# The first expert stage of a two-layer transformer kernel: 32 pairs and 7 single tiles instead of 28 and 15, with a tile table of sixteen segments

## The reference

```
logits = einsum('btd,ed->bte', x, router_w)
top_vals, top_idx = top_k(logits, 2);  top_w = softmax(top_vals)
h = square(relu(einsum('nd,edh->enh', xf, w1)))
y = einsum('enh,ehd->end', h, w2)
out = sum over the two choices of top_w * y[choice, row]
x = x + attention0(layernorm(x)) + experts0(layernorm(x))
```

## Time and profile before

| | |
|---|---|
| median of 3 runs | 760.42 us (760.25, 760.42, 761.84) |
| span of the profiled execution | 761.9 us |
| TensorE busy | 716.6 us, 94% |
| VectorE busy | 564.2 us, 74% |
| ScalarE busy | 438.9 us, 58% |
| GpSimd busy | 456.4 us, 60% |
| share of TensorE in the chain that ended last | 84% |
| DMA | 113.96 MB, mean 150 GB/s |

### The profile page before, as it was taken

How to read it: one execution, slowest core, us unless ns; L and a number is a source line. 1 busy time by engine, 2 the same in 40 slices (tenths; PEclk the granted TensorE clock), 3 DMA queues, 4 the chain that set the end, 5 groups by cost and what they waited for, 6 DMA issues and landing times.

```text
span 761.9 us, 19272 instructions
## 1 busy us (share of the span) xinstructions
PE 716.6 (94%) x6112; PEld 631.8 (83%) x6112; DVE 564.2 (74%) x1280; ACT 438.9 (58%) x928; POOL 456.4 (60%) x577
## 2 busy tenths in 40 slices
PE   6999999799999999999998999899999899999994
PEld 4888864699999999999977999777778678888883
DVE  4888874788778887788758886589998766676632
ACT  5444525576776776755526888456677664544411
POOL 3676777889798696988422323024376645665363
PEclk9999999999999999999999999799999999999997
DMA  9799752343454344453168996145457755666342
GB/s 255 209 266 277 210 148 75 90 134 108 132 151 123 112 125 138 124 136 107 48 184 274 300 288 184 29 95 123 107 110 194 222 194 133 147 148 147 54 56 28
DMA packets 151103, 113.96 MB, mean 150 GB/s; under 512 B 59359, under 2 KB 141282, under 8 KB 151012
## 3 DMA queue, kind: packets, MB, share of 16 engines
q1 hardware_dynamic: 137812, 86.94, 41.0%
q0 software_dynamic: 12624, 25.35, 13.3%
q10 hardware_dynamic: 576, 0.53, 0.3%
HBM read 68.68 MB, written 40.80 MB: 144 GB/s over the span
## 4 chain that ended last, share of the span: by engine, by line
PE 84%; DVE 7%; issue 3%; ACT 2%; DMA 1%; POOL 1%; SPq 0%; POOLq 0%; DVEq 0%; ACTq 0%
PE banks L917 13%; PE bank L1173 11%; PE bank L882 11%; PE banks L1184 5%; PE bank L973 5%; PE banks L747 4%; PE banks L812 4%; PE bank L893 4%; PE bank L754 3%; PE bank L1080 3%; PE bank L1063 3%; PE banks L990 3%; PE bank L865 2%; PE bank L1052 2%; PE banks L801 2%
## 5 line engine op out<-in xcount | busy, mean ns | idle before, releaser
L917 PE MATMUL banks<-r_split,rt_split 128*128 x852 | 111.0, 285 | 1.1 <-issue 0.9
L917 PEld LDWEIGHTS banks<-r_split,rt_split 128*128 128x128 f32 x852 | 105.1, 191 | 1.9 <-issue 1.9
L2247 POOL DMA_INDIRECT ults_by_choice_and_token<-rw,y_id x71 | 79.1, 1114 | 45.1 <-ACT rw L1361 34.6
L1173 PE MATMUL bank<-r_split 128*128 128x512 f32 x384 | 89.6, 391 | 1.3 <-issue 1.1
L882 PE MATMUL bank<-wqkv_split,rt_split 128*128 128x256 f32 x560 | 86.9, 286 | 4.2 <-DVE rt_split L1767 4.1
L1173 PEld LDWEIGHTS bank<-r_split 128*128 128x128 f32 x384 | 71.4, 188 | 16.3 <-issue 1.9
L2346 POOL DMA_INDIRECT out_x<-r,idx x32 | 50.2, 1568 | 52.9 <-DVE r L2105 45.2
L882 PEld LDWEIGHTS bank<-wqkv_split,rt_split 128*128 128x128 f32 x560 | 76.0, 189 | 5.9 <-DVE rt_split L1767 5.4
L2216 POOL DMA_INDIRECT rows_by_expert<-rw,slots x64 | 68.0, 1062 | 18.6 <-issue 9.8
L1767 DVE TENSOR_TENSOR rt_split<-r,rt_split 128x512 fp32r<-128x512 f32 x56 | 62.1, 1149 | 18.7 <-ACT rt_split L1290 16.6
L1792 DVE TENSOR_TENSOR rt_split<-rw,rt_split 128x512 fp32r<-128x512 f32 x71 | 63.1, 919 | 6.3 <-ACT rt_split L1354 6.0
(11 more groups left out here) (275 smaller groups left out, 1759.3 us busy)
## 6 DMA issues: line engine op xcount, KB each, us to landing
rt<-in_w SPq DMA_DIRECT2D x24, 512.0 KB, 4.8
rw<-rows_by_expert SPq DMA_DIRECT2D x71, 128.0 KB
r<-in_w SPq DMA_DIRECT2D x16, 512.0 KB, 7.4
rt<-ults_by_choice_and_token SPq DMA_DIRECT2D x32, 256.0 KB, 4.1
rw<-in_x SPq DMA_DIRECT2D x16, 256.0 KB, 4.8
rw<-in_sin_q SPq DMA_DIRECT2D x32, 128.0 KB
rw<-x_layer SPq DMA_DIRECT2D x16, 256.0 KB
x_plus_bias<-rw SPq DMA_DIRECT2D x16, 256.0 KB, 3.5
```

The source lines that it names most:

```text
L917: last = pe.matmul(bank[6 + t % 2][:, 0:D], hidden_T(h, t, c), w[:, ds(e2, 1), o + c * D:o + (c + 1) * D], start=n == 0, stop=n == 3 * HC - 1)
L1173: last = pe.matmul(bank[2 * (hb % 2) + k][:, :], w[:, o:o + P], x[:, s.par, c, :], start=n == 0, stop=n == 3 * DC - 1)
L2247: pool.indirect_dma_start(y0_d[:, :], bass.IndirectOffsetOnAxis(y_id[:, t:t + 1].bitcast(I32), 0), c_y[:, t % XB, :], None, bounds_check=l ...
```

## The change

ND goes from 28 to 32: T1 is 64, there are 32 pairs and 7 singles. The table has sixteen segments: for each expert its full pairs, and then for each expert its odd tile counted as two places, the tile and an empty one behind it. The first 64 places are the pairs, what remains of the odd tiles is halved into singles. The chain on VectorE has 21 small operations where it had 15, its four comparisons and products work on 16 segments instead of 8, and so does the reduction. Each expert's end gets 256 rows of zeros instead of 128. Three memsets more run on GpSimd at the start. The split of the next layer's weights moves from T1 + 4 to T1 + 1 and from T1 + 6 to T1 + 3, that is from 60 to 65 and from 62 to 67.

```
--- before.py
+++ after.py
@@ -147,7 +147,6 @@
         xT_all = r3f[:, 0:DC * N].rearrange("p (c n) -> p c n", c=DC)
         v_all = r2[:, :].rearrange("p (h t n) -> p h t n", h=2, t=NT)
         pid0 = sb("pid0", [P, 1])
-        one8 = sb("one8", [P, E])
         m_all = sb("m_all", [P, NB, 2, D])
         hot1_hi = r3[:, 0:NT * E * 32].rearrange("p (c n) -> p c n", c=NT)
         hot1_lo = r3[:, NT * E * 32:NT * E * 64].rearrange("p (c j e m) -> p c j e m", c=NT, j=2, e=E)
@@ -184,15 +183,17 @@
         prod = scratch([TOPK * GT * E])
         upto, span_e = scratch([E]), scratch([GT * E], BF16)
         end_r = sb("end_r", [P, E], I32)
-        n_i, n_f, d_pair, d_one = scratch([3 * E], I32), scratch([E]), scratch([E]), scratch([E])
-        pair_n, pair_incl, u2, s_incl = scratch([E]), scratch([E]), scratch([E + 1]), scratch([E])
+        n_i, n_f = scratch([3 * E], I32), scratch([E])
+        seg, covered, one16 = scratch([2 * E]), scratch([2 * E]), scratch([2 * E])
+        seg_incl, start, apart = scratch([2 * E]), scratch([2 * E + 1]), scratch([2 * E])
+        step_to = scratch([2 * E])
         base_f, headmask = scratch([ST0]), scratch([2, P // 2])
         top_v, top_i = scratch([NT, E]), scratch([NT, E]).bitcast(U32)
         base_i = scratch([ST0], I32)
         assert taken[0] <= 2 * DC * H, taken[0]
         taken[0] = 2 * DC * H
         taken[0] += 8 * D
-        past, past_d = scratch([E, ST0]), scratch([E, ST0])
+        past = scratch([2 * E, ST0])
         taken[0] = 2 * DC * H
         a_kr, a_t, a_v = scratch([2, 2 * D]), scratch([2 * D]), scratch([3, 2 * D])
         o = taken[0]
@@ -302,7 +303,7 @@
         x1_out, x1_late = [sem(f"x1_stored_{i}") for i in range(4)], sem("last_x1_stored")
         xn1_out, xb1_out = sem2("xn1_stored"), sem2("xb1_stored")
 
-        XB, ND = 4, 28
+        XB, ND = 4, 32
         T1 = 2 * ND
         NTR = ST0 - ND
         c_xg = work([XB, D], reset=True)
@@ -563,8 +564,8 @@
                 load_xq(i)
             sp.wait_ge(table_r, 1)
             for e in range(0, E, 2):
-                r = sp.value_load(end_r[0:1, e:e + 1], min_val=0, max_val=(REG - 1) * P)
-                sp.dma_start(xs0_d[ds(r, P), :], zeros).then_inc(zero_out, 16)
+                r = sp.value_load(end_r[0:1, e:e + 1], min_val=0, max_val=(REG - 2) * P)
+                sp.dma_start(xs0_d[ds(r, 2 * P), :].rearrange("(j p) n -> p j n", p=P), over_mid(zeros, 2)).then_inc(zero_out, 16)
             for i in range(4):
                 sp.wait_ge(sc0_out[i], 16 * TOPK * GT * NG // 4)
             sp.wait_ge(table_r, 2)
@@ -1317,8 +1318,8 @@
             copy_q(0)
             act.wait_ge(table_r, 1)
             for e in range(1, E, 2):
-                r = act.value_load(end_r[0:1, e:e + 1], min_val=0, max_val=(REG - 1) * P)
-                act.dma_start(xs0_d[ds(r, P), :], zeros).then_inc(zero_out, 16)
+                r = act.value_load(end_r[0:1, e:e + 1], min_val=0, max_val=(REG - 2) * P)
+                act.dma_start(xs0_d[ds(r, 2 * P), :].rearrange("(j p) n -> p j n", p=P), over_mid(zeros, 2)).then_inc(zero_out, 16)
             for g in range(1, NQ):
                 if g == NQ - 1:
                     high_rows_T(0)
@@ -1385,7 +1386,7 @@
                 if t < ST0:
                     relu0(t)
                     high0(t)
-                if t == T1 + 4:
+                if t == T1 + 1:
                     act.wait_ge(consts_b, 16 * 9)
                     act.activation(wq1_hi[:, :, :], wqkv1_s[:, :, :], ACT.Copy).then_inc(wq1_r, 1)
 
@@ -1724,24 +1725,32 @@
             link(dve.tensor_scalar(n_i[:, E:2 * E], n_i[:, 0:E], 7, None, ALU.logical_shift_right))
             link(dve.tensor_scalar(n_i[:, 2 * E:3 * E], n_i[:, 0:E], 8, None, ALU.logical_shift_right))
             link(dve.tensor_copy(n_f, n_i[:, E:2 * E]))
-            link(dve.tensor_copy(pair_n, n_i[:, 2 * E:3 * E]))
-            link(dve.tensor_scalar(pair_n, pair_n, 2.0, None, ALU.mult))
-            link(dve.tensor_tensor_scan(pair_incl, one8[:, :], pair_n, 0.0, ALU.mult, ALU.add))
-            link(dve.tensor_tensor(u2[:, 0:E], pair_n, pair_incl, ALU.subtract))
-            link(dve.tensor_scalar(u2[:, 0:E], u2[:, 0:E], float(T1), 0.0, ALU.add, ALU.max))
-            link(dve.tensor_tensor(u2[:, 0:E], u2[:, 0:E], pair_n, ALU.min))
-            link(dve.memset(u2[:, E:E + 1], 0.0))
-            link(dve.tensor_tensor(d_one, n_f, u2[:, 0:E], ALU.subtract))
-            link(dve.tensor_tensor_scan(s_incl, one8[:, :], d_one, float(T1), ALU.mult, ALU.add))
-            link(dve.tensor_tensor(d_one, u2[:, 1:E + 1], n_f, ALU.subtract))
-            link(dve.tensor_scalar(d_one, d_one, float(SPAN), None, ALU.add))
-            link(dve.tensor_scalar(d_pair, pair_n, -1.0, float(SPAN), ALU.mult, ALU.add))
-            for lo, hi, incl, d in ((0, T1, pair_incl, d_pair), (T1, ST0, s_incl, d_one)):
-                link(dve.tensor_tensor(past[:, :, lo:hi], over_mid(iota_t[:, lo:hi], E), over_last(incl, hi - lo), ALU.is_ge))
-                link(dve.tensor_tensor(past_d[:, :, lo:hi], past[:, :, lo:hi], over_last(d, hi - lo), ALU.mult))
-            link(dve.tensor_reduce(base_f, past_d.rearrange("p e t -> p t e"), AX, ALU.add))
+
+
+
+            link(dve.tensor_scalar(seg[:, 0:E], n_i[:, 2 * E:3 * E], 2.0, None, ALU.mult))
+            link(dve.tensor_tensor(seg[:, E:2 * E], n_f, seg[:, 0:E], ALU.subtract))
+            link(dve.tensor_scalar(seg[:, E:2 * E], seg[:, E:2 * E], 2.0, None, ALU.mult))
+            link(dve.tensor_tensor_scan(seg_incl, one16, seg, 0.0, ALU.mult, ALU.add))
+            link(dve.tensor_tensor(covered, seg, seg_incl, ALU.subtract))
+            link(dve.tensor_scalar(covered, covered, float(T1), 0.0, ALU.add, ALU.max))
+            link(dve.tensor_tensor(covered, covered, seg, ALU.min))
+            link(dve.tensor_copy(start[:, E:2 * E], seg[:, 0:E]))
+            for part, lo, hi in (("pairs", 0, T1), ("singles", T1, ST0)):
+                if part == "singles":
+                    link(dve.tensor_copy(start[:, 0:E], covered[:, 0:E]))
+                    link(dve.tensor_tensor(seg, seg, covered, ALU.subtract))
+                    link(dve.tensor_scalar(seg[:, E:2 * E], seg[:, E:2 * E], 0.5, None, ALU.mult))
+                    link(dve.tensor_tensor_scan(seg_incl, one16, seg, float(T1), ALU.mult, ALU.add))
+                link(dve.tensor_tensor(step_to, start[:, 1:2 * E + 1], start[:, 0:2 * E], ALU.subtract))
+                link(dve.tensor_tensor(step_to, step_to, seg, ALU.subtract))
+                link(dve.tensor_tensor(step_to, step_to, apart, ALU.add))
+                link(dve.tensor_tensor(past[:, :, lo:hi], over_mid(iota_t[:, lo:hi], 2 * E), over_last(seg_incl, hi - lo),
+                                       ALU.is_ge))
+                link(dve.tensor_tensor(past[:, :, lo:hi], past[:, :, lo:hi], over_last(step_to, hi - lo), ALU.mult))
+            link(dve.tensor_reduce(base_f, past.rearrange("p e t -> p t e"), AX, ALU.add))
             link(dve.tensor_tensor(base_f, base_f, iota_t[:, :], ALU.add))
-            link(dve.tensor_scalar(base_f[:, T1:ST0], base_f[:, T1:ST0], u2[:, 0:1], -float(T1), ALU.add, ALU.add))
+            link(dve.tensor_scalar(base_f[:, T1:ST0], base_f[:, T1:ST0], start[:, 0:1], -float(T1), ALU.add, ALU.add))
             dve.tensor_scalar(tile_r[:, :], base_f, float(P), None, ALU.mult).then_inc(table_r, 1)
             link(dve.tensor_copy(base_i, base_f))
             link(dve.tensor_scalar(base_i, base_i, 6, None, ALU.logical_shift_right))
@@ -1825,7 +1834,7 @@
                     low0(t - 1)
                 if t < ST0:
                     square0(t)
-                if t == T1 + 6:
+                if t == T1 + 3:
                     dve.wait_ge(wq1_r, 1)
                     dve.tensor_tensor(wq1_lo[:, :, :], wqkv1_s[:, :, :], wq1_hi[:, :, :].bitcast(F32), ALU.subtract)\
                        .then_inc(wq1_r, 1)
@@ -2176,7 +2185,10 @@
             pool.iota(span_e, pattern=[[0, GT], [SPAN, E]], base=0, channel_multiplier=0, allow_small_or_imprecise_dtypes=True)
             pool.iota(upto, pattern=[[-SPAN * P, E]], base=P - 1, channel_multiplier=0, allow_small_or_imprecise_dtypes=True)
             pool.iota(iota_t[:, :], pattern=[[1, ST0]], base=0, channel_multiplier=0, allow_small_or_imprecise_dtypes=True)
-            pool.memset(one8[:, :], 1.0)
+            pool.memset(one16, 1.0)
+            pool.memset(start, 0.0)
+            link(pool.memset(apart, float(SPAN)))
+            link(pool.memset(apart[:, E - 1:E], float(SPAN - E * SPAN)))
             pool.memset(hot_pad, 0.0)
             pool.memset(zeros[:, 0:D], 0.0)
             pool.memset(zeros[:, D:D + 1].bitcast(I32), 1 << 20)
```

## The result

The changed kernel takes 767.38 us, the median of 7 runs (764.8 to 769.8), beside 760.42 us for 7 runs of the kernel before (758.54 to 765.25). The ratio is 1.0075, with a 95% interval of 1.0056 to 1.0095: slower, by about 5.7 us; the two medians differ by 7.0. The forecast was 759.5 us, within 757.9 to 763.2, and most likely no difference.

The account below looks back on a forecast made before the run. TensorE holds most of the span, and in front waits on VectorE's table chain. Pairs -2.8, passage -0.7, front +2.6 gave -0.9 us: 759.5 against the median 760.42, range 757.9 to 763.2.

Parts of the forecast that it names:

- Sum: +3.3 us, between 3.0 and 3.6: VectorE's table chain before the key-value product: small operations +1.3, large ones +1.15, reduction +0.9 us.
- Net +2.6, between 2.3 and 2.9: Front: TensorE pays the table chain's +3.3 us at 113.77 and gets back 0.68 us at 131.09.
- The 0.68 us: TensorE's wait at 131.09 before the first row transposes; claimed to be regained, as TensorE would arrive after the loads.
- The clock: the rival that came true: Wait at 113.77 growing to 3.9 us lowers TensorE's clock: +3 to +5 us, middle +4, 763.5; chance 0.22.
- one fall beside the start: Argument against the clock's fall: only one beside the start is shown, where work before was thin for longer.
- nearer to certain: Chance of TensorE's clock falling by the skill's rule that idleness throttles the array to half; the prediction gave 0.22.
- The 5.1 us: Cost of a low-clock stretch of 10.24 us on TensorE behind the wait, taken as half its length.
- The stage: Expert stage: eight singles becoming four pairs gain 2.8 us, the passage to singles 0.7; gain of 3.5 us.
- I take 6.14, since GpSimd has fewer rotations left at steps 56 to 63: Time of each new pair step: 6.14 us, 24.6 for four against 27.4 for eight singles, gain 2.8.
- The passage: From last pair's product to first single's: 1.7 of 7.64 us are extra; between 0 and 1.7 return, 0.7 taken.
- the delay moves into another pair: Lower bound of the gain at the passage from pairs to singles: 0 us, where rotations 56 and 58 now fall.
- no cost of the zero rows: Front: 256 zero rows cost nothing; rival that they hold up the scatters, at most 0.9 us more, 760.4, chance 0.13.

Follow-up runs that it names:

- first and second profile: Profiled executions of the changed kernel: the first with front 39.1 us, wait 4.12; the second from running it once more, front 42.7, wait 6.20, ratio 1.0063.
- filler: Five extra matmuls in TensorE's wait: 1.0046 against 1.0082 on the kernel before with its table reduction made four times; 1.0012 against 1.0069 with GpSimd's first query rotation held.
- pairs only: Kernel before with 32 pairs, 7 singles and the moved weight split, old table and 128 zero rows: ratio 0.9968 to the kernel before.
- rotation first: Changed kernel with the last key rotation on VectorE moved ahead of the table: ratio 0.9965 to the kernel before.
- changed again: The changed kernel itself run once more, in another set: ratio 1.0063 to the kernel before.
- GpSimd later: Changed kernel with GpSimd's first query rotation waiting until VectorE's table is done: ratio 1.0069 to the kernel before.
- zero rows: Changed kernel with 128 zero rows to an expert instead of 256: ratio 1.0077 to the kernel before.
- table only: Changed kernel with the stage of before (28 pairs, 15 singles, old weight split), keeping the new table and 256 zero rows: ratio 1.0102 to the kernel before.
- before with rotation first: Kernel before with the last key rotation on VectorE moved ahead of its own table: ratio 0.9983 to the kernel before.
- before with longer table: Kernel before with the reduction at the end of its table made four times instead of once: ratio 1.0082 to the kernel before.

## Why the prediction was wrong

**The sum of the front: mis-sized.** The chain's own terms ("Sum: +3.3 us, between 3.0 and 3.6") were nearly right. Small operations +1.6 (forecast +1.3; one tensor_scalar took 0.43), the elementwise ones +1.2 (+1.15), the reduction 2.20 for 1.17, which is +1.0 (+0.9: its cost is nearly all in its elements). To the reduction's end +3.8 instead of +3.3. What the sum lacked is what comes behind it: GpSimd's multiplications, which in the trace of before begin at 119.85, long after the table's end, meet the end of the longer table in five of the seven profiles of kernels with this table in its own order, and add 0.7 to 2.1 us (from the reduction's end to the last table operation 2.0 to 3.5 us, alone 1.34). I priced the new operations by their rows and did not ask what a chain that ends 4 us later runs into. Together with the clock this is the step that failed: "Net +2.6, between 2.3 and 2.9" for the front, which grew by 4.0 to 7.6 us. The 0.68 us came back as said.

**The clock: the rival that came true.** It had 0.22, and it is the largest single part of the miss. "It decides from a wait between 2.7 and 3.9 us" holds nearly: in the front there was no fall after 1.46 us, a fall within 2.72, falls in all waits of 4.1 to 6.3. Its price was +3 to +5; measured are 1.4 and some 3.0 us at the wait (first and second profile), 2.8 and 4.4 us by ratios with and without filler, as uncertain as said above, and 0.004 of mean clock, which over 762 us is 3.0, an estimate. Not the mechanism but the weight was wrong. I set "one fall beside the start" against it, where the earlier trace rows had shown that idle time lowers the clock and nothing spoke for an exception. By the Trainium skill's rule (TensorE: Matmul & The Clock Gate, Part 1), weighed in the prediction as "nearer to certain", 763.5 would have been the forecast. The 5.1 us worked out from the 10.24 us of the earlier trace rows were too much: TensorE works 2.9 to 6.0 us at the low clock here.

**The stage: right in sign, half as much again as was measured.** Forecast -3.5. The six profiles with 32 pairs, rotations in place and no extra matmuls (changed, pairs only, rotation first, changed again, GpSimd later, zero rows) average 242.3 us; those with 28 pairs (before, table only, before with rotation first, before with longer table) 244.7: -2.4. The step that failed is "I take 6.14, since GpSimd has fewer rotations left at steps 56 to 63". Fewer, but two, and each makes a pair late. (Three of the four kernels with extra matmuls took longer, 244.5 and 245.6 with 32 pairs and 248.1 with 28; why isn't known.) The passage gave back its full 1.5 us, and pairs 26 to 29 lost 2.7 (27.26 for 4 x 6.14), 1.7 of it in the three pairs that the rotations delay and 1.0 in pair 26. The bound "the delay moves into another pair" was written down for this, but only as an end of the range.

**Right:** no cost of the zero rows was seen, the 0.68 and the wait at the passage went, the seven singles start 3.43 us apart, TensorE had nothing to hide the table.

**A slip without effect:** the prediction set the profile's span, 761.9, beside the runs' times, as 1.5 above the median. As a time it is 763.6, 3.2 above. Only the difference of -0.9 was carried over to the median, so the 759.5 stands.

**The account.** The front of the second profile closes to 0.3: the chain to the rotation's end +5.6 (15.80 for 10.19), clock +3.0, -0.7 regained, in all +7.9, measured 42.7 - 35.1 = +7.6. In the first it was +3.5 + 1.4 - 0.7 = +4.2, measured +4.0. The five profiles with the new table in its own order, extra matmuls and GpSimd's later start left out, have a mean front of 41.2, for 35.1 and 35.6 before: +5.8. Stage -2.4. Together +3.4, while the medians say +5.2 (767.4 for 762.2) and +7.0, the ratios +4.8 and +5.7. Executions scatter by 10 us, so one profile of each kernel can't close this; 1 to 2 us are not placed. The two halves measured in themselves say the same: +7.9 and -2.5.

## What to carry to other kernels

When a chain on another engine gets longer in front of TensorE, its price is the added wait, and the clock behind it, and whatever its end newly overlaps: here +3.8, some +1.4 to +3 and up to +2.1 us. Ask first whether the waiting result depends on the chain at all: the last key rotation didn't, and two lines moved took away the wait and everything that hung on it. Work that is bound to step numbers must be looked at again when the number of steps of a kind changes.

## What the runs showed of the hardware

In the front, TensorE's granted clock fell from 1.00 to 0.50 during or just behind each of the eight waits for the key rotation of 2.72 to 6.29 us, one to a profile, and stayed at 1.00 after the one of 1.46 us. After 4.12 us of waiting TensorE worked 2.9 us at the low clock, after 6.20 us 6.0. The clock can fall after the engine has started again (0.49, 0.48, then 0.64 us for the same matmuls). Ahead of pair 1 the length of the idle time does not tell: it was 2.1 to 2.7 us in the 13 profiles with a fall (4.29 to 4.63 us for the product) and 2.3 to 2.8 us in the four without (3.09 to 3.12).

A VectorE tensor_scalar on 7 elements took 1.33 to 1.40 us beside GpSimd's multiplications, in four profiles, and 0.23 alone; one on 71 integers 0.65 and 0.20. For operations this short, what runs beside them is the price: the one of 1.33 us spans three multiplications of 0.45.

A reduction over a strided axis took 1.17 us for 568 elements and 2.20 for 1136: 1.8 ns for each added element, where an added element of an elementwise operation took 1.1 ns.
